# Attention over a graph: who issues the stores of the exponentials

## The reference

```
h = x @ weight
h_norm = h / max(norm(h), 1e-8)
sim = h_norm @ h_norm.T
attn = softmax(sim + log(adj + 1e-8), axis=1)
out = attn @ h + bias
```

## Time and profile before

| what | value |
|---|---|
| median of 3 executions | 2351.0 us (2350.78 to 2352.5) |
| the profiled execution | 2352.74 us |
| its span (first to last instruction) | 2350.9 us, mean granted TensorE clock 0.999 |
| busy: PE / DVE / ACT / POOL | 2307.7 / 1716.5 / 1133.3 / 138.4 us |
| DMA: mean busy share, rate | q1 (issued by SP) 89.2% of 16 engines' span; 309 GB/s over the span |
| attention pass | about 745 to 1345 us of the span |

### The profile page before, as it was taken

One profiled execution on the slowest core, in us unless ns is written; L12 is line 12 of the kernel. 1 busy time (PEld: TensorE's weight loads), 2 busy tenths in 40 slices (PEclk: granted clock), 3 DMA queues, 4 the chain that ended last, 5 costly groups with the idle time before them and its releaser, 6 DMA issues.

```text
span 2350.9 us, 62654 instructions
## 1 busy us (share of the span) xinstructions
PE 2307.7 (98%) x24536; PEld 1936.7 (82%) x24536; DVE 1716.5 (73%) x2734; ACT 1133.3 (48%) x1821; POOL 138.4 (6%) x114
## 2 busy tenths in 40 slices
PE   7999999999999999999999999999999999999999
PEld 7888887666665677777778799999988888899998
DVE  7887867677676777778888876776776766667665
ACT  6634443445444555655555545545554444433332
POOL 2211101101100000000000000000000000000000
PEclk9999999999999999999999999999999999999999
DMA  8699998888987999989989899899898898999997
GB/s 286 222 359 338 354 359 300 258 269 273 280 265 206 266 273 296 283 260 304 323 289 314 288 373 328 299 336 327 305 339 323 311 353 309 336 344 382 369 380 290
DMA packets 291738, 726.86 MB, mean 309 GB/s; under 512 B 76704, under 2 KB 109728, under 8 KB 258848
## 3 DMA queue, kind: packets, MB, share of 16 engines
q1 hardware_dynamic: 291328, 724.42, 89.2%
q10 hardware_dynamic: 288, 0.79, 0.1%
HBM read 574.64 MB, written 138.41 MB: 303 GB/s over the span
## 4 chain that ended last, share of the span: by engine, by line
PE 83%; DVE 9%; issue 4%; ACT 1%; POOL 1%; DMA 1%; DVEq 0%; SPq 0%; POOLq 0%; ACTq 0%
PE acc L913 9%; PE acc L916 8%; PE acc L918 8%; PE acc L917 8%; PE acc L938 7%; PE acc L942 7%; PE acc L941 6%; PE acc L914 5%; PE acc L928 4%; PE acc L931 4%; PE acc L930 4%; PE psS L1154 2%; PE psS L1156 2%; PE psS L1155 2%; DVE alo L1668 1%
## 5 line engine op out<-in xcount | busy, mean ns | idle before, releaser
L916 PE MATMUL acc<-right,ahi 128*128 128x258 f16 x1536 | 419.8, 273 | 3.4 <-DVE o L1681 2.1
L918 PE MATMUL acc<-right,alo 128*128 128x258 f16 x1536 | 419.5, 273 | 0.0
L917 PE MATMUL acc<-right,ahi 128*128 128x256 f16 x1536 | 418.8, 273 | 0.0
L938 PE MATMUL acc<-left,ahi 128*128 128x128 f16 x1536 | 270.6, 219 | 6.2 <-DVE alo L1672 6.0
L941 PE MATMUL acc<-left,ahi 128*128 128x128 f16 x1536 | 270.5, 219 | 0.0
L942 PE MATMUL acc<-left,alo 128*128 128x128 f16 x1536 | 270.4, 219 | 0.0
L1538 ACT ACTIVATE ahi<-en 128x512 f16<-128x512 f32 x256 | 160.2, 626 | 83.5 <-DVE en L1944 79.9
L916 PEld LDWEIGHTS acc<-right,ahi 128*128 128x128 f16 x1536 | 150.3, 98 | 36.9 <-DVE alo L1959 6.6
L913 PE MATMUL acc<-left,ahi 128*128 128x512 f16 x512 | 180.2, 379 | 0.0
L913 PE MATMUL acc<-left,en 128*128 128x512 f16 x512 | 180.2, 379 | 0.0
L938 PE MATMUL acc<-left,adj 128*128 128x128 f16 x1024 | 178.1, 219 | 0.0
(11 more groups left out here) (245 smaller groups left out, 6537.9 us busy)
## 6 DMA issues: line engine op xcount, KB each, us to landing
adj<-in_adj_t SPq DMA_DIRECT2D x192, 512.0 KB, 5.9
adj<-ready SPq DMA_DIRECT2D x96, 1024.0 KB, 7.5
en<-ready SPq DMA_DIRECT2D x96, 1024.0 KB, 7.5
adj<-in_adj_t SPq DMA_DIRECT2D x32, 1024.0 KB, 8.3
en<-in_adj_t SPq DMA_DIRECT2D x32, 1024.0 KB, 8.8
en<-ready SPq DMA_DIRECT2D x64, 512.0 KB, 5.2
en<-sent SPq DMA_DIRECT2D x46, 512.0 KB, 6.6
sent<-en SPq DMA_DIRECT2D x90, 256.0 KB, 4.4
```

Source lines behind the costliest of these rows:

```text
L916: nc.tensor.matmul(acc[:, b, 0:n], hi, m[:, jb, 0:n], start=first, stop=False)
L917: nc.tensor.matmul(acc[:, b, 0:F], hi, m[:, jb, LO:LO + F], start=False, stop=False)
L918: return nc.tensor.matmul(acc[:, b, 0:n], lo, m[:, jb, 0:n], start=False, stop=last)
L938: nc.tensor.matmul(to, hi[:, rows], bhi[:, cols], start=first and i % 2 == 0 and b == 0 and k == 0, stop=False, skip_group_check=True)
```

## The change

`send` moves from SP's program to ACT's. Nothing is computed otherwise, and the bytes and the number of DMAs stay the same. On SP, the call with its wait for exp_ready is gone, from between `att_half` and `fetch_exp`. On ACT, it comes at even j, behind the exponential of j and the high part of j - 1, and ahead of the s4 part and of the stages of `ATT_PLACES`: at j = 2H + 2 for half H, and at j = 0 of the next group for the last half.

```diff
-            def send(g, H):
-
-                sp.wait_ge(exp_ready, exp_no(g, HALF * H + HALF - 1))
-                k = H % 2 * HALF
-                rows = sent_rows(g, H // 2)
-                to = sent[rows:rows + 2 * P, k * GR // 2:(k + HALF) * GR // 2]
-                for e in range(2):
-                    sp.dma_start(to[e * P:(e + 1) * P, :].rearrange("p (b n) -> p b n", b=HALF),
-                                 exp_slot(g, H).rearrange("p (b n) -> p b n", b=HALF)[:, :, e * GR // 2:(e + 1) * GR // 2])\
-                        .then_inc(exp_sent[H % 8], 16)
...
                             att_half(g, H)
-                            before = (g, H - 3) if H >= 3 else (g - 1, H - 3 + NH)
-                            if before[0] >= 0 and is_sent(*before):
-                                send(*before)
                             after = (g, H + 1) if H + 1 < NH else (g + 1, 0)
...
+            def send(g, H):
+
+                act.wait_ge(exp_ready, exp_no(g, HALF * H + HALF - 1))
+                k = H % 2 * HALF
+                rows = sent_rows(g, H // 2)
+                to = sent[rows:rows + 2 * P, k * GR // 2:(k + HALF) * GR // 2]
+                for e in range(2):
+                    act.dma_start(to[e * P:(e + 1) * P, :].rearrange("p (b n) -> p b n", b=HALF),
+                                  exp_slot(g, H).rearrange("p (b n) -> p b n", b=HALF)[:, :, e * GR // 2:(e + 1) * GR // 2])\
+                        .then_inc(exp_sent[H % 8], 16)
...
                         hi_of_numerators(g - 1, NB - 1)
+                    if j >= HALF and j % HALF == 0 and is_sent(g, j // HALF - 1):
+                        send(g, j // HALF - 1)
+                    elif g > 0 and j == 0 and is_sent(g - 1, NH - 1):
+                        send(g - 1, NH - 1)
                     if g * NB + j - 1 in S4_AT:
```

## The result

| kernel | median us | lowest to highest | runs |
|---|---|---|---|
| before | 2352.05 | 2350.78 to 2352.95 | 6 |
| changed | 2360.76 | 2356.43 to 2366.11 | 6 |

The ratio is 1.0037, 95% interval 1.0027 to 1.0048: slower by 8.7 us, and the times spread over 10 us where they spread over 2 before. The time lies above the range of 2349.5 to 2356.5. The profiled execution of the changed kernel is the fastest of its six (2356.43 us, span 2354.6), so its profile shows 3.7 us of the loss.

The account below looks back on a forecast made before the run. PE was taken to bound the kernel. 0 (SP) + 0.4 (ACT) + 0 (DMA) gave +0.4 us on the profiled 2352.74; forecast median 2351.5 us, range 2349.5 to 2356.5.

Parts of the forecast that it names:

- What bounds the kernel: Attention pass: PE bounds it, busy 583.52 of 600.00 us; at most 16.5 us to win, none named by a DMA.
- The cost on ACT: 112 issues added to ACT's queue at 56 even j: up to 0.4 us in all.
- the hidden end: ACT's queue runs ahead of its datapath, so a pair costs 0 to 0.1 us where ACT is critical, nothing elsewhere.
- all four critical places: Groups 0 (twice), 1 and 2, where PE's weight loads wait for ACT's low part without slack; a store pair precedes each.
- rival A: ACT's datapath waits for the issue, 0.9 us at each critical place: 2354.6 to 2355.5 us; chance 0.22.
- When the stores go: Stores on ACT go up to 2 us before the high part, or some 3 us later than before; costed at 0.
- SP: Some 52 us of issue time and the waits at L715 leave SP's queue; 0 us for the end.
- Rival B: The two queues hinder each other at issue, as beside SP's transposes: 2356 to 2363 us, say 2359; chance 0.12.
- What would show it: Profile signs: ACT issues of about 0.45 us beside running activations, "h" unmoved, SP's waits moved to the adj loads.
- the sign named for being wrong: In the pass, PE's busy time stays and its idle time grows by over 4 us, or shrinks by that.

Follow-up runs that it names:

- e2: The changed kernel with the stores of halves 11 to 15 of each group back on SP; 2352.58 us, ratio 1.0003.
- e3: The kernel before with only the stores of halves 11 to 15 of each group issued by ACT; 2359.72 us, ratio 1.0031.
- e8: The kernel before, all stores on SP, but each behind the fetch and other DMAs of its half; 2356.98 us, ratio 1.0024.
- e6: The kernel before with another HBM layout, stores in pieces of 4 KB and fetches in pieces of 1 KB; 2352.29 us, ratio 1.0002.
- e7: The changed kernel with only the store of each group's last half (H = 15) back on SP; 2352.17 us, ratio 1.0004.
- e10: The changed kernel with SP waiting for the landing of each group's last store before its next fetch; 2358.74 us, ratio 1.0028.

## Why the prediction was wrong, point by point

- **What bounds the kernel**: right. PE, with 16.5 us to win at most, and none of it with SP's stores. No run with stores on ACT was faster than before. (The largest wait of SP's queue was read without its second row, 26.4 us for exponentials in left; nothing rests on it.)
- **The cost on ACT**: right, the hidden end. The issues lie beside running activations, "h" came 0.11 us later at the place looked at, and e2 with 25 pairs on ACT, all four critical places among them, costs nothing (interval 0.9993 to 1.0012). With this, rival A falls.
- **When the stores go**: wrong in part. ACT's queue was less far ahead than the "up to 2 us" of the prediction: the store of half 6 went 0.4 us ahead of the high part, 2.2 us later than before measured against the work. It was harmless there. The last store of each group went 0.84 us behind its exponential, where SP had issued it 0.02 us behind, and that is a part of what its fetch lost.
- **The step that failed** is in the paragraph on when the stores go: "The fetches of the next group are closer, since their slots were last used by stores of the group's end (see the rivals). I cost them at 0. Bytes and packets are the same." A landing of 4.3 us was taken over from the store's old place, though that number was made by the place: on SP's queue the store stood ahead of 512 KB of fetch, 512 KB for s4 and s2 and 512 KB of adj, which now run beside it. For the last store of a group the landing went from a mean of 4.1 to 7.4 us, and the way from its issue to the fetch that it releases from 4.5 to 8.1 us. The small slack had been found, 1.8 us in group 5, but was set only against a delay of the issue of 1.3 us (rival A), never against one of the landing. Put at nothing too, without a word, was what a wait of PE does to its clock: behind the longest one, 3.39 us, it cost an estimated 2.9 more.
- **SP**: the sentence "If a fetch was held up behind a store, it now goes earlier" had the wrong sign. The fetch of half 5 of group 5 went 6.4 us later. The store held it up by its landing, not by its place in the queue.
- **Rival B** named a time, 2359, that the measurement comes near to, but by another mechanism. Its price was 2 to 3 us for a pair on ACT at critical places; the issue measured 0.427 us in the median, and e2, with the pairs at all critical places, cost nothing. The rows show the transpose of group 1 and the issues of ACT in the midst of it:

```profile
869.25 4.12 SPq L649 DMA_TRANSPOSE hT<-hsp  x1
...
871.18 0.38 ACTq L1513 DMA_DIRECT2D sent<-left  x1
871.56 0.62 ACT L1535 ACTIVATE ahi<-en 128x512 f16<-128x512 f32 x1
871.59 1.50 ACTq L1513 DMA_DIRECT2D sent<-left  x1
```

  One of them took its usual 0.38 us, the second 1.50 us and was done before the transpose's issue ended at 873.37; ACT's next exponential started at 873.60 and had waited for PE. So an issue on ACT needn't wait out a transpose. In the Trainium skill (page "Perfetto Trace Analysis", section "DMA Instruction — HWDGE (DVE, Sync)") the lock of the descriptor generator ends before the profiled duration does. These rows agree with a lock that covers only a part of the 4.12 us, and don't show how large a part.
- **What would show it**: the sign named for being wrong, idle time of PE grown by 4 us with the same busy time, is nearly what the profile shows (3.5 us). SP's waits were to move from L715 to the adj loads with about the same total; those grew by 78 us (153.0 to 230.9), but the wait for the landing at L729 grew by 108, and that is the one that mattered.
- **The range** reached too little to the slow side: it had a cost of issue in it and no cost of landing. The spread of 10 us of the changed kernel had no counterpart in the forecast either. One source is on record, PE's clock. Some of the slower profiled executions have more stretches at 0.50 between 755 and 1370 us (e3 at 2361.76 us has three of 3.4 us, the first two behind waits of 2.98 and 2.51 us for fetched exponentials; e8 at 2360.30 has two in the pass behind waits of 2.63 and 2.07, and one at its end), each worth up to 1.7 us and 3.4 for e8's last, while the profiles of e2, e6 and e7, without loss, have none there. Not every wait brings one: the kernel before waits 2.72 us at the end of the pass and keeps its clock. Whether the two queues also meet differently in each execution was not tested.

## What to carry to other kernels

A time to landing belongs to a place in a queue as much as to a transfer: before moving a DMA to another queue, list what will run beside it, ask who waits for its landing (a slot to be freed as well as data), and set the slack there against a landing nearly twice as long (4.1 to 7.4 us here). Two us of PE's waiting can cost more than two, if its clock falls with them. A long wait in an issuing queue is neither a cost nor a gain by itself: 105 us at SP's stores were worth nothing, and in e7 95 us of waiting for stores cost nothing, while one store in eight, at the place without slack, cost 6 us. If stores are moved to ACT, leave the ones that free a buffer for the next load ahead of that load in its own queue.

## What the runs showed of the hardware

ACT issued a pair of 256 KB stores in 0.9 us while its datapath ran the activations ahead of it; the activation behind came 0.11 us later at the place shown, and 25 such pairs cost nothing measurable (e2). The landing of a group's last stores grew from 4.1 to 7.4 us in the mean when 1.5 MB of SP's transfers ran beside them from another queue, and was 4.4 us on the same second queue with none of SP's issued behind them until they had landed (e10). Pieces of 4 KB in place of 1 KB made no measurable difference to the kernel's time. TensorE's granted clock fell to 0.50 for 3.4 to 6.8 us behind several, not all, of its waits of 1.8 to 3.4 us. DMAs of 8-byte pieces, 28,672 pieces with 0.23 MB in all, lengthened the kernel by 92 us, and SP's 256 KB stores beside them took 11.3 us to land in place of 4.4.
